# A hybrid layer stack on one core: GpSimd's clears and splits reordered, the rotation's sums moved to GpSimd

## The chip, the cores and the metric

The kernel runs on one core of one Trainium2 chip. The metric is the device time of one execution in microseconds. The engines are named as in the profile: PE is TensorE, PEld its weight load, DVE is VectorE, ACT is ScalarE, POOL is GpSimd and SP is SyncE, which issues all the transfers.

## The reference

The input x has 4 batches of 256 tokens with 256 channels. Four parts are added to it in turn, each computed from a layer norm of the current x:

```
x = x + attn_a(layernorm(x))     # 16 heads of 128, causal softmax attention with biases
x = x + ffn(layernorm(x))        # per-token int8 quantisation, product with an int8 256x256 weight
x = x + attn_b(layernorm(x))     # 16 heads of 128, 64 memory slots a head
x = x + ffn(layernorm(x))
```

attn_b works on rotated queries and keys. The rotation splits each head's 128 features in two halves:

```
rope(x) = concat(x1 * cos - x2 * sin, x2 * cos + x1 * sin)
s = clip(hs @ Ws1.T @ Ws2.T + bs2);  z = cumlogsumexp(s)
ok = exp(-z) * (tril(q k^T) @ exp(s));  qv = softmax(ok)
o = tril((qv * exp(-z)) @ exp(s)^T) @ v
out = (rmsnorm(o) * silu(g)) @ Wo.T
```

## The kernel before

Every engine has one instruction list written out by hand, and semaphores join the lists. So an instruction that waits holds up all that stand behind it on its engine. Heads are worked in 8 pairs. A loop over pairs (`Fori(0, PAIRS - 1)` with `a_body`, later with `b_body`) is followed by a last pair that is written out. Inside a body, b runs over the 4 batches, and while batch b's attention is computed, the projections for the other half of the tokens (512 tokens at a time) are put between its products as filler. Projections of q and k, and those of v and the gate in attn_b, are done in three products of split numbers: ACT writes the high part (`split_head`, line 530), POOL subtracts it from the raw weights for the low part (`split_tail`, line 380, and `split_out_tail`, line 385, for the output weights). For x the high part comes from ACT (`transposed`, line 537) and the low part from DVE (`tail`, line 820).

Four norms are numbered 0 to 3. DVE makes the statistics (`ln_stats`, 804 and 807), POOL the reciprocal root (`ln_rsqrt`, 372 and 374), DVE the scaled rows (`ln_scale`, 813). PE transposes them (`transpose_x`, 1199), and ACT copies the transposed rows out, first a plain copy (536), then the high part (537).

At the start POOL clears five buffers (`oT_hi`, `oT_lo`, `wo_hi`, `wo_lo`, `accT`, lines 401 to 407) just after the first low parts, while DVE scales batches 2 and 3 of norm 0. PE does the first of eight projection tasks, then transposes batches 2 and 3, then does the other seven. Between the two attentions POOL splits the weights of v and gate and clears `wo_hi`, `wo_lo` and `accT` again. Each ffn runs as `ffn_quant` (826 to 840), transposes (1212), a product (1221), `ffn_out` (849 and 855, which leaves float16 rows), and `ffn_add` on POOL (391).

The rotation in attn_b: ACT copies the projection with its two halves exchanged into `rot_s` (666, 667), POOL multiplies that by the sines in place (`rope_mul`, 439), DVE multiplies the projection in PSUM by the cosines into `rot` (`b_rope_cos`, 992), and DVE adds the two into qT or kT (`b_rope_add`, 999). `rot` and `rot_s` have one buffer for head 0 and one for head 1, shared by q and k. PE's next score products wait for all four sums of their phase (`b_rope`), and PE's reuse of a projection bank waits for the cosine product that reads it.

The gate's norm weight is folded into the output weights by ACT (`wos`, line 722). In the loop its low part is taken by POOL. In the last pair PE's `out_proj` (1371) multiplies by `wos` itself, after waiting for `b_wos`:

```
if last:
    pe.wait_ge(b_wos, PAIRS)
    out_proj(b_, b, wos)
```

Of the kernel before, what the change touches and what calls it, by code (L numbers as in the profile page):

```python
# [29 lines left out]
F32 = mybir.dt.float32  # L30
# [41 lines left out]
def layer_kernel(nc, x_in, a_wq, a_bq, a_wk, a_bk, a_wv, a_bv, a_wo, a_bo,  # L72
                 b_wq, b_wk, b_wv, b_wg, b_wo, b_ws1, b_ws2, b_bs2, b_gw,
                 f_w, f_ws, f_bias, consts, out):
    with ExitStack() as ctx:
# [111 lines left out]
        cast_done = sem("cast_done")  # L187
        gwh_done = sem("gwh_done")
# [173 lines left out]
        def _(pool):  # L362
# [3 lines left out]
            g.memset(ws2[:, :], 0.0).then_inc(init_done, 1)  # L366

# [31 lines left out]
            def zero_outputs():  # L399

                g.memset(wo_hi[:, :, :].bitcast(F32), 0.0)
                g.memset(wo_lo[:, :, :].bitcast(F32), 0.0)
                return g.memset(accT[:, :, :], 0.0)
# [24 lines left out]
            ln_rsqrt(2, 1)  # L428
            split_tail(b_, 0, 2)

            pool.wait_ge(a.y_acc, y_count(B - 1))
            zero_outputs().then_inc(b_.y_acc, 1)

            def rope_mul(n, m, k):
# [5 lines left out]
                                ).then_inc(b_rotmul, 1)  # L440

# [20 lines left out]
            def b_body(i, last):  # L462
                x = i * B
                for b in range(B):
# [4 lines left out]
                    if b % 2 == 0:  # L469
# [8 lines left out]
                        if rest:  # L478
                            rope_mul(n("q0"), 0, 0)
                            rope_mul(n("q1"), 0, 1)  # L480
                        if nxt:
                            slots(x + b + 1, (b + 1) % B)
                        if rest:
                            rope_mul(n("k0"), 1, 0)
                    else:
                        if last and b == 3:
                            ln_rsqrt(3, 2)
                        if rest:
                            rope_mul(n("k1"), 1, 1)
# [13 lines left out]
            for j, (m, k) in enumerate(((0, 0), (0, 1), (1, 0), (1, 1))):  # L503
                rope_mul(slot_done(0, 0, B_TASKS.index(ROPES[j])), m, k)
                if j == 0:
                    ffn_add(0, 2)
                if j == 1:
                    ffn_add(0, 3)
                    ln_rsqrt(2, 2)
                    ln_rsqrt(2, 3)  # L510
# [10 lines left out]
        def _(act):  # L521
# [10 lines left out]
            def transposed(m, b, bank):  # L532
# [3 lines left out]
                s.activation(xT[:, :, cols], src, ACT.Copy)  # L536
                s.activation(xT_hi[:, :, cols], src, ACT.Copy).then_inc(xts[m].hi, 1)

# [1140 lines left out]
```

## Time and profile before

| | us |
|---|---|
| median of 3 runs (lowest to highest) | 839.63 (838.05 to 842.48) |
| time of the profiled execution | 837.9 |
| its span | 836.1 |
| PE busy | 775.7 (93%) |
| DVE busy | 592.8 (71%) |
| ACT busy | 432.7 (52%) |
| POOL busy | 277.3 (33%) |

The span goes from the first instruction to the last one. Busy time is the share in which an engine executes; a busy PE is not necessarily at its highest clock. A line's time gives the start, then the duration.

### The profile page before, as it was taken

The page shows a single profiled execution, that of the slowest core. Times are in us where ns is not written, and L with a number is a line of the kernel's source. Part 1 is how long each engine was busy: PE and PEld are TensorE (multiplying, and loading weights), DVE is VectorE, ACT ScalarE, POOL GpSimd, SP SyncE. Part 2 cuts the span into 40 slices and gives each one's busy share as a digit, 9 for nine tenths or more (in the row PEclk, how much of TensorE's full clock was granted, in tenths as well). Part 3 has the DMA queues.
Part 4 walks back from the last instruction along what each step waited for, and adds up shares of the span by engine and source line. Part 5 has one row for each costly group of instructions (what it writes and reads, how often), then busy time and mean ns, then how long its engine had stood idle before and what let it go on. Part 6 is the DMA issues. An engine that isn't in the chain of part 4 may idle for free.

```text
span 836.1 us, 14186 instructions
## 1 busy us (share of the span) xinstructions
PE 775.7 (93%) x4428; PEld 655.5 (78%) x4428; DVE 592.8 (71%) x1500; ACT 432.7 (52%) x1184; POOL 277.3 (33%) x285
## 2 busy tenths in 40 slices
PE   3999999999999995689999999999999999999963
PEld 2788888888888884368888888888888888888752
DVE  6455554555555448888888878888888788887776
ACT  3555555555555543356656566565565665565320
POOL 6110010101001004535635446356354463553231
PEclk9999999999999999799999999999999999999996
DMA  7010101101010200100100101001001010000001
GB/s 246 1 51 0 50 12 38 50 0 50 0 50 12 63 1 13 51 2 13 51 1 13 50 1 63 0 13 50 0 13 50 12 50 0 13 0 0 1 1 51
DMA packets 23653, 23.74 MB, mean 28 GB/s; under 512 B 2369, under 2 KB 23361, under 8 KB 23506
## 3 DMA queue, kind: packets, MB, share of 16 engines
q1 hardware_dynamic: 23634, 23.51, 8.9%
q8 instruction: 10, 0.16, 0.1%
q14 instruction: 9, 0.07, 0.0%
HBM read 22.45 MB, written 1.05 MB: 28 GB/s over the span
## 4 chain that ended last, share of the span: by engine, by line
PE 87%; DVE 8%; ACT 1%; issue 1%; POOL 1%; DMA 1%; SPq 0%; ACTq 0%; DVEq 0%
PE ps L1247 21%; PE ps L1453 11%; PE ps L1354 6%; PE ps L1252 6%; PE ps L1275 5%; PE ps L1465 3%; PE ps L1318 3%; PE ps L1359 3%; DVE xn L813 3%; PE ps L1490 2%; PE ps L1294 2%; PE ps L1477 2%; PE ps L1507 2%; PE ps L1509 2%; PE ps L1508 2%; PE ps L1466 2%
## 5 line engine op out<-in xcount | busy, mean ns | idle before, releaser
L1247 PE MATMUL ps<-xT_hi,w_hi 128*128 128x512 f32 x256 | 110.2, 431 | 4.4 <-DVE rot L992 2.5
L380 POOL TENSOR_TENSOR w_lo<-w_raw,w_hi 128x512 fp32r<-128x512 f32 x32 | 40.7, 1282 | 217.3 <-ACT w_hi L530 217.3
L1247 PE MATMUL ps<-xT_hi,w_lo 128*128 128x512 f32 x256 | 101.6, 397 | 0.0
L1247 PE MATMUL ps<-xT_lo,w_hi 128*128 128x512 f32 x256 | 101.2, 395 | 0.0
L1022 DVE TENSOR_TENSOR wt<-ps,const 128x384 f32<-128x384 f32 x128 | 68.3, 555 | 41.8 <-PE ps L1466 21.9
L439 POOL TENSOR_TENSOR rot_s<-rot_s,const 128x512 f32<-128x512 f32 x64 | 81.9, 1291 | 16.1 <-ACT rot_s L667 16.1
L574 ACT ACTIVATE wt<-wt,negmax 128x128 f32<-128x128 f32 (+1 forms) x128 | 56.6, 443 | 36.1 <-DVE negmax L889 36.1
L877 DVE TENSOR_TENSOR v<-ps,bv_b 128x256 f32<-128x256 f32 x64 | 26.9, 422 | 59.5 <-PE ps L1252 59.4
L1252 PE MATMUL ps<-wv,xT 128*128 128x256 f32 x256 | 63.1, 380 | 1.0 <-DVE v L877 1.0
L686 ACT ACTIVATE v<-ps 128x256 f32<-128x256 f32 x64 | 24.4, 381 | 73.4 <-PE ps L1453 73.2
L1011 DVE RECIPROCAL enz<-zs 128x128 f32<-128x128 f32 x64 | 60.3, 942 | 0.0
L1247 PEld LDWEIGHTS ps<-xT_hi,w_hi 128*128 128x128 f32 x256 | 48.9, 191 | 13.9 <-issue 2.9
L1247 PEld LDWEIGHTS ps<-xT_hi,w_lo 128*128 128x128 f32 x256 | 48.7, 190 | 11.2
L459 POOL TENSOR_TENSOR qp<-oke,enz 128x256 f32<-128x256 f32 x32 | 23.6, 736 | 101.6 <-ACT oke L691 101.6
L1453 PE MATMUL ps<-wc_hi,xT_hi 128*128 128x512 f32 x128 | 56.5, 441 | 0.0
L884 DVE TENSOR_TENSOR wt<-ps,const 128x128 f32<-128x128 f32 x64 | 18.3, 286 | 53.1 <-PE ps L1275 53.1
L992 DVE TENSOR_TENSOR rot<-ps,const 128x512 f32<-128x512 f32 x64 | 43.6, 681 | 16.1 <-ACT rot_s L667 16.1
L1247 PEld LDWEIGHTS ps<-xT_lo,w_hi 128*128 128x128 f32 x256 | 49.1, 192 | 6.9
L666 ACT ACTIVATE rot_s<-ps 64x512 f32<-64x512 f32 x64 | 38.0, 594 | 30.1 <-PE ps L1247 27.6
L1453 PE MATMUL ps<-wc_hi,xT_lo 128*128 128x512 f32 x128 | 50.8, 397 | 0.0
L1453 PE MATMUL ps<-wc_lo,xT_hi 128*128 128x512 f32 x128 | 50.7, 396 | 0.0
L591 ACT ACTIVATE wt<-ps 128x384 f32<-128x384 f32 x64 | 30.1, 486 | 39.6 <-PE ps L1294 39.6
(160 smaller groups left out, 2140.8 us busy)
## 6 DMA issues: line engine op xcount, KB each, us to landing
w_raw<-a_w_q SPq DMA_DIRECT2D x8, 256.0 KB, 3.2
w_raw<-a_w_k SPq DMA_DIRECT2D x8, 256.0 KB, 3.8
wv<-a_w_v SPq DMA_DIRECT2D x8, 256.0 KB, 2.5
wo<-a_w_o SPq DMA_DIRECT2D x8, 256.0 KB, 3.3
w_raw<-b_Wq SPq DMA_DIRECT2D x8, 256.0 KB, 2.6
w_raw<-b_Wk SPq DMA_DIRECT2D x8, 256.0 KB, 3.3
wc<-b_Wv SPq DMA_DIRECT2D x8, 256.0 KB, 3.5
wc<-b_Wg SPq DMA_DIRECT2D x8, 256.0 KB, 4.0
```

Of the source, the lines that this page charges most:

```text
L380: g.tensor_tensor(lo[:, :, :], raw[:, :, :], hi[:, :, :].bitcast(F32), ALU.subtract).then_inc(ph.w_lo, 1)
L439: g.tensor_tensor(ap, ap, const[:, col:col + T].unsqueeze(1).to_broadcast([P, 2, T]), ALU.mult).then_inc(b_rotmul, 1)
L574: last = s.activation(wt[:, h, lo:hi], wt[:, h, lo:hi], ACT.Exp, bias=negmax[:, h, r:r + 1], scale=(1.0, -1.0)[r], accum_out=rowsum[:, h, ...
L666: s.activation(rot_s[0:M, k, :], PJ[bank][M:P, :], ACT.Copy)
L992: d.tensor_tensor(rot[:, k, :].rearrange("p (b t) -> p b t", b=2), PJ[n[0]].rearrange("p (b t) -> p b t", b=2), const[:, col:col + T].unsq ...
L1011: d.reciprocal(enz[:, HT * half + k, :], zs[:, k * P:(k + 1) * P]).then_inc(b_recip_done, 1)
L1022: d.tensor_tensor(dst, src[:, 0:384], tri3, ALU.mult).then_inc(done, 1)
L1247: ins = mm(PJ[n[0]], w[:, m, c, h * P:(h + 1) * P], x[:, c, cols], start=(t == 0), stop=(t == len(terms) - 1))
L1252: ins = mm(bank_ap, xT[:, c, tile * P:(tile + 1) * P], w[:, c, :], start=(c == 0), stop=(c == C - 1))
L1275: ins = mm(W_[h][:, lo:hi], qT[:, h, t0 + r * P:t0 + (r + 1) * P], kT[:, h, t0:t0 + hi - lo], start=True, stop=True)
L1354: mm(Y_, w[:, h, c * P:(c + 1) * P], oT_hi[:, half, h, :], start=(h == 0 and w is wo_hi), stop=False)
L1453: ins = mm(PJ[bank], x[:, c, tile], w[:, c, :], start=(c == 0 and t == 0), stop=(c == C - 1 and t == 2))
```

## The change

In words, by place:

- POOL at the start: `wo_hi`, `wo_lo` and `oT_hi` are cleared ahead of the first `ln_rsqrt`, `oT_lo` between the first two. `split_tail(a, 0, 0)` waits until DVE has scaled batches 0 and 1, `split_tail(a, 0, 1)` until all are scaled, and the clear of `accT` comes after it.
- The start on the other engines: ACT's plain copies of x leave `transposed` for norm 0 and come later (`x_copy`). DVE takes the low parts of batches 0 and 1 before the statistics of batch 3. PE does the four q and k projections without a break, then transposes batches 2 and 3. DVE takes their low parts between the evacuations of v.
- Between the attentions: POOL waits until six tiles of norm 1 are scaled before it clears `wo_hi` and `wo_lo`, and splits v's and gate's weights only after all of `ffn_quant(0, ...)`. `accT` is cleared after the first `slots`. Two `ffn_add` go from POOL to DVE (`add_ffn`), and DVE's list there is reordered.
- In attn_b's loop: the four sums of a phase go from DVE to POOL (`rope_add`), behind the sine products. DVE's and ACT's lists are reordered: `b_recip` of tile 0 moves to the odd steps, the exponential of `oke` goes ahead of k0 and et, the copy to `wos` goes behind k0, and the two weight splits of the odd step change places with squares and copies.
- At the end: `ffn_quant(1, 2)` is cut into `ffn_range` and `ffn_round` with the add of batch 3 and its statistics between, `ffn_out(1, 2)` goes behind `ffn_quant(1, 3)`, and POOL holds `ffn_add(1, 1)` until batch 2 is scaled.

The diff, cut to its core:

```diff
             g.memset(ws2[:, :], 0.0).then_inc(init_done, 1)
+            g.memset(wo_hi[:, :, :].bitcast(F32), 0.0)
+            g.memset(wo_lo[:, :, :].bitcast(F32), 0.0)
+            g.memset(oT_hi[:, 1, :, :].bitcast(F32), 0.0)
...
-            for b in range(B):
-                ln_rsqrt(0, b)
-                if b == 1:
-                    split_tail(a, 0, 0)
+            ln_rsqrt(0, 0)
+            g.memset(oT_lo[:, 1, :, :].bitcast(F32), 0.0)
+            ln_rsqrt(0, 1)
+            pool.wait_ge(norms[0].xn, 4)
+            split_tail(a, 0, 0)
+            ln_rsqrt(0, 2)
+            ln_rsqrt(0, 3)
+            pool.wait_ge(norms[0].xn, TILES)
             split_tail(a, 0, 1)
...
-            g.memset(oT_hi[:, 1, :, :].bitcast(F32), 0.0)
-            g.memset(oT_lo[:, 1, :, :].bitcast(F32), 0.0)
-            zero_outputs()
-            pool.wait_ge(norms[0].xn, TILES)
+            g.memset(accT[:, :, :], 0.0)
...
             ln_rsqrt(2, 1)
+            pool.wait_ge(norms[1].xn, 6)
+            pool.wait_ge(a.y_acc, y_count(B - 1))
+            g.memset(wo_hi[:, :, :].bitcast(F32), 0.0)
+            g.memset(wo_lo[:, :, :].bitcast(F32), 0.0)
+            pool.wait_ge(ffns[0].qb, B)
             split_tail(b_, 0, 2)
-            pool.wait_ge(a.y_acc, y_count(B - 1))
-            zero_outputs().then_inc(b_.y_acc, 1)
...
+            def rope_add(r1, k, m, half):
+                pool.wait_ge(b_rotcos, r1)
+                pool.wait_ge(b_rotmul, r1)
+                g.tensor_tensor((qT, kT)[m][:, k, half * HALF:(half + 1) * HALF], rot[:, k, :], rot_s[:, k, :],
+                                ALU.add).then_inc(b_rope, 1)
...
                             rope_mul(n("q0"), 0, 0)
                             rope_mul(n("q1"), 0, 1)
+                            rope_add(4 * phase + 1, 0, 0, 1 - b // 2)
+                            rope_add(4 * phase + 2, 1, 0, 1 - b // 2)
                         if nxt:
                             slots(x + b + 1, (b + 1) % B)
                         if rest:
                             rope_mul(n("k0"), 1, 0)
+                            rope_add(4 * phase + 3, 0, 1, 1 - b // 2)
+                            rope_mul(n("k1"), 1, 1)
+                            rope_add(4 * phase + 4, 1, 1, 1 - b // 2)
...
             slots(0, 0)
+            g.memset(accT[:, :, :], 0.0).then_inc(b_.y_acc, 1)
...
+            pool.wait_ge(norms[3].xn, 6)
             ffn_add(1, 1)
...
-                        if b == 0:
-                            act.wait_ge(b_.wo_ld, i * 16 + 16)
-                            s.activation(wos[:, :, :], wo[:, :, :], ACT.Copy, scale=gwh[:, 0:1]).then_inc(b_wos, 1)
...
-                        if rest:
-                            t("k0")
                         if nxt:
                             b_okexp_step(x + b + 1)
+                        if rest:
+                            t("k0")
+                        if b == 0:
+                            act.wait_ge(b_.wo_ld, i * 16 + 16)
+                            s.activation(wos[:, :, :], wo[:, :, :], ACT.Copy, scale=gwh[:, 0:1]).then_inc(b_wos, 1)
...
-            for b in range(2, B):
-                ln_stats(0, b, x_ld[b], 16)
-            for b in range(B):
-                tail(0, b, 2 + b)
-                if b == 1:
-                    ln_scale(0, 2)
-                    ln_scale(0, 3)
+            ln_stats(0, 2, x_ld[2], 16)
+            tail(0, 0, 2)
+            tail(0, 1, 3)
+            ln_stats(0, 3, x_ld[3], 16)
+            ln_scale(0, 2)
+            ln_scale(0, 3)
...
-                            b_recip(n(3), half, 0)
-                            b_rope_add(4 * phase + 1, 0, 0, half)
...
             b_clip_s(n0(0), 0)
             ffn_out(0, 2)
+            ffn_out(0, 3)
             b_rope_cos(n0(1), 0, 0)
-            ffn_out(0, 3)
+            b_recip(n0(3), 0, 0)
             b_rope_add(1, 0, 0, 0)
+            add_ffn(0, 2)
+            add_ffn(0, 3)
+            ln_stats(2, 2, ffns[0].acc, 3)
             b_rope_cos(n0(2), 1, 0)
...
-            ffn_out(1, 2)
+            ffn_round(1, 2)
             ln_scale(3, 3)
             ffn_quant(1, 3)
+            ffn_out(1, 2)
             ffn_out(1, 3)
...
             for j in range(NA):
-                if j == 1:
+                if j == 4:
+                    pe.wait_ge(x_plain, 2)
                     transpose_x(0, 2, 4)
                     transpose_x(0, 3, 5)
-                if j == 4:
-                    pe.wait_ge(xts[0].lo, 4)
                     a_scores(0, 0, [(0, 2), (1, 2)])
                 a_task((j % 2, j // 2, None), j, 0, 0)
+            pe.wait_ge(xts[0].lo, 4)
+            pe.wait_ge(x_plain, 4)
```

## Rows read from the trace of the kernel before

**Rows 1.** Busy time in one stretch: length, PE, PEld, DVE, ACT, POOL, then clock, DMA.
```profile
500.00:550.00 50.00, 49.92 (x315) 43.02 (x315) 40.78 (x85) 29.35 (x84) 24.45 (x24) 1.00 0.08 26
```

**Rows 2.** PE alone by stretch: length, busy time, granted clock, DMA share, GB/s.
```profile
21.00:22.00 1.00, 1.00 (x4) 0.50 0.00 0
...
336.00:338.00 2.00, 0.05 (x1) 0.50 0.00 0
...
358.00:360.00 2.00, 2.00 (x6) 0.50 0.01 4
```

**Rows 3.** Instructions in order of time at the start: start, duration, engine, line.
```profile
8.47 1.73 DVE L813 TENSOR_SCALAR xn<-acc,mv,rstd 128x256 f32<-128x256 f32 x2 [0.61 <-POOL rstd L374]
...
13.13 6.86 DVE L813 TENSOR_SCALAR xn<-acc,mv,rstd 128x256 f32<-128x256 f32 x4
...
17.08 1.81 POOL L403 MEMSET accT<- 128x2048 f32 x1
```

**Rows 4.** The chain that ended last, at the start and in the loop: start, duration, what.
```profile
19.41 1.76 PE ps L1199 x8
21.17 5.18 PE ps L1247 x18
...
27.20 0.91 PE ps L1275 x4
...
505.12 1.39 PE ps L1453 x6
...
532.65 1.39 PE ps L1453 x6
```

**Rows 5.** Instructions in order of time between the two attentions.
```profile
334.18 0.70 DVE L813 TENSOR_SCALAR xn<-acc,mv,rstd 128x256 f32<-128x256 f32 x2
335.49 6.06 DVE L813 TENSOR_SCALAR xn<-acc,mv,rstd 128x256 f32<-128x256 f32 x4 [0.60 <-POOL rstd L374]
...
347.67 0.69 DVE L1005 TENSOR_SCALAR clip_buf<-ps 128x512 f32<-128x512 f32 x1
...
353.02 1.50 DVE L855 TENSOR_TENSOR y<-y,fb_b 128x512 f16<-128x512 f32 x1
354.45 1.74 DVE L999 TENSOR_TENSOR qT<-rot,rot_s 128x512 f32<-128x512 f32 x1
...
338.64 1.80 POOL L403 MEMSET accT<- 128x2048 f32 x1
...
364.68 0.70 PE L1465 MATMUL ps<-qT,kT 128*128 128x256 f32 x2 [1.36 <-DVE kT L999]
```

**Rows 6.** Instructions in order of time in one half of a pair of the second loop.
```profile
502.56 0.69 DVE L999 TENSOR_TENSOR kT<-rot,rot_s 128x512 f32<-128x512 f32 x1
...
503.64 0.60 PE L1465 MATMUL ps<-qT,kT 128*128 128x256 f32 x2
...
518.89 2.52 POOL L439 TENSOR_TENSOR rot_s<-rot_s,const 128x512 f32<-128x512 f32 x2
524.93 0.74 POOL L459 TENSOR_TENSOR qp<-oke,enz 128x256 f32<-128x256 f32 x1 [3.53 <-ACT oke L691]
...
527.22 0.59 ACT L667 ACTIVATE rot_s<-ps 64x512 f32<-64x512 f32 x1
```

**Rows 7.** Instructions in order of time in the last pair's first step.
```profile
760.44 0.73 ACT L722 ACTIVATE wos<-wo,gwh 128x512 f32<-128x512 f32 x1
...
773.22 0.59 ACT L667 ACTIVATE rot_s<-ps 64x512 f32<-64x512 f32 x1
...
772.42 1.02 PE L1371 MATMUL ps<-wos,clip_buf 128*128 128x256 f32 x4
```

**Rows 8.** Instructions in order of time at the end.
```profile
817.58 1.57 DVE L813 TENSOR_SCALAR xn<-acc,mv,rstd 128x256 f32<-128x256 f32 x2
...
824.35 0.69 DVE L855 TENSOR_TENSOR y<-y,fb_b 128x512 f16<-128x512 f32 x1
...
831.20 0.88 DVE L849 SCALAR_TENSOR_TENSOR y<-ps,qsc,ws_b 128x256 f32<-128x256 f32 x2 [2.43 <-PE ps L1221]
```

More of the change, by code:

```diff
@@ L555, in _ @@
             transposed(0, 1, 3)
+            x_copy(0, 2)
+            x_copy(1, 3)
             act.wait_ge(bias_ld, 16 * 4)
@@ L625, in _ @@
                 a_qk((f % 2, f // 2, f + 1), A_TASKS[f], 0, 0)
-                if f == 0:
-                    transposed(0, 2, 4)
-                    transposed(0, 3, 5)
+            transposed(0, 2, 4)
+            transposed(0, 3, 5)
             a_exp_step(0)
+            x_copy(2, 4)
+            x_copy(3, 5)
             act.wait_ge(small_ld, 16 * 7)
@@ L746, in b_body @@
                             t("k1")
+                            t("c0")
+                        if last and b == 3:
+                            ffn_copy(1, 1)
                         if b == 1 and not last:
@@ L749, in b_body @@
                         if rest:
-                            t("c0")
                             t("c1")
-                        b_squares(x + b)
-                        if last and b == 3:
-                            ffn_copy(1, 1)
                         if b == 1 and not last:
@@ L757, in b_body @@
                             split_head(b_, i + 1, 0)
+                        b_squares(x + b)
                         if rest:
                             t("c2")
-                        if b == 1 and not last:
-                            split_head(b_, i + 1, 1)
                         act.wait_ge(b_ogt_ps, x + b + 1)
@@ L767, in b_body @@
                             s.activation(oT_hi[:, b // 2, :, (b % 2) * T:(b % 2 + 1) * T], src, ACT.Copy).then_inc(b_.o_hi, 1)
+                        if b == 1 and not last:
+                            split_head(b_, i + 1, 1)
+                        if nxt:
+                            b_okexp_step(x + b + 1)
                         if rest:
                             t("et")
-                        if nxt:
-                            b_okexp_step(x + b + 1)
             act.wait_ge(init_done, 3)
@@ L982, in _, with b_rope_cos @@
             tail(1, 0, ffns[0].banks[0])
+            tail(1, 1, ffns[0].banks[1])
             ffn_quant(0, 2)
-            tail(1, 1, ffns[0].banks[1])
             ln_scale(1, 3)
             ffn_quant(0, 3)
-            def b_rope_cos(n, k, m):
+            def b_rope_cos(n, k, m, phase=0):
                 dve.wait_ge(b_.proj_evac[n[0]], n[1] + 1)
+                if not (isinstance(phase, int) and phase == 0 and m == 0):
+                    dve.wait_ge(b_rope, 4 * phase + 2 * m + k - 1)
                 col = (K_QCOS, K_COS)[m]
@@ L1115, in b_body @@
                         if rest:
-                            b_rope_cos(n(5), 1, 1)
-                            b_rope_add(4 * phase + 4, 1, 1, half)
+                            b_gate(n(6), phase, 0, half)
+                            b_recip(n(3), half, 0)
                         if last and b == 3:
@@ L1120, in b_body @@
                         if rest:
-                            b_gate(n(6), phase, 0, half)
+                            b_gate(n(7), phase, 1, half)
                             b_recip(None, half, 1)
+                        if last and b == 3:
+                            ffn_out(1, 0)
                         if nxt:
                             b_scores(x + b + 1)
-                        if rest:
-                            b_gate(n(7), phase, 1, half)
-                        if last and b == 3:
-                            ffn_out(1, 0)
                         b_gated(x + b, b)
@@ L1135, in b_body @@
                             out_tail(b_, x + b, b, O_)
+                        if rest:
+                            b_recip(None, half, 2)
                         if last and b == 3:
@@ L1138, in b_body @@
                             ln_scale(3, 2)
-                            ffn_quant(1, 2)
-                        if rest:
-                            b_recip(None, half, 2)
+                            ffn_range(1, 2)
                         (add_y if last else add_group)(b_, x + b, b)
```

64 lines of the change are left out of this document (34 added, 30 removed).

## The prediction, made before the changed kernel ran

> **What bounds the kernel now.** I first read the busy time by stretch [rows 1]. In the second attention's loop PE is busy for 49.92 of 50 us while DVE has 40.78 and POOL 24.45. There PE's own work sets the time, and what is taken from DVE is worth nothing unless it closes a gap in PE. PE alone by stretch shows where it is otherwise [rows 2]: near 21 us it works at half the clock, near 336 us it stands, near 358 us it again works at 0.50, shortly after a stop of 2.5 us. So I read those places, the last pair and the end in order of time.
>
> At the start two scalings of the norm (line 813) take 1.73 us, and then four take 6.86 [rows 3]. Between the attentions two take 0.70 and four take 6.06 [rows 5]. The instruction is the same, so the long ones are not working but held. In both places POOL runs without a break beside them: at the start a weight split and then clears up to 17.08 + 1.81 = 18.89, in the middle a split and clears up to 338.64 + 1.80 = 340.44. The scalings end 1.1 us after POOL does, the time of the remaining ones. PE's transposes of batches 2 and 3 wait for them until 19.41 [rows 4]. So this wait is on the path twice. At the end two scalings take 1.57, with one POOL add beside them, and the two of batch 3 the same [rows 8].
>
> The Trainium skill ("SBUF — State Buffer", section "SBUF: two separate sides") has VectorE in a two-port mode and GpSimd share a port pair that is locked for a whole instruction. By that rule alone a scaling would wait for one POOL instruction at most. The trace agrees on the lock and not on the turn-taking: the scaling waited through six POOL instructions.
>
> **The start, -6.0 us.** POOL's clears go to where it idles, and the first split waits for the scalings.
> - The second pair of scalings takes 0.70 instead of 1.73: -1.0. One plain copy (0.60, as long as ACT's 0.59 in [rows 6]) leaves ACT's path to the second high part: together about -1.5, so PE starts its first projection at 11.75 instead of 13.27.
> - PE then does all 24 products of the four tasks without the stop up to 19.41. At the high clock six take 1.39 us (0.232 each); 18 took 5.18 [rows 4], partly at the low level. At the clock of 0.50 [rows 2] six would take 2.6 (0.43 each), not quite twice the 1.39. Before, about 12 of the 24 ran at the low level. I take 12 again: 12 x 0.43 + 12 x 0.232 = 7.9, so to 19.7, plus 0.9 for eight transposes: scores at 20.5 against 27.20, -6.7. With 9 low products it is -7.3, with all 24 low (10.3, and transposes of 1.76) -3.4.
> - The low parts of batches 2 and 3 now lie on DVE between the v evacuations (2 x 0.60), and the loop waits for ACT's last plain copy (0.60). That costs about 0.7 back: -6.0. POOL's second split ends near 15.7, before PE needs it near 17. The bias add on POOL (4.6 us) ends before the softmax's scalings.
>
> The bounds: -7, and -3.
>
> **Between the attentions, -3.0 us.** The four scalings shrink from 6.06 to 1.4, but the second batch still has to be transposed, copied twice and subtracted: the low part ends near 339.3, and two quantisations and a scaling (5.1 us) follow. The clip starts at 344.45 instead of 347.67: -3.2. Behind it both `ffn_out` now stand ahead of the first cosine, which then comes only 0.7 earlier (PE's k0 near 350.9 instead of 352.9). The reciprocal, the first sum, the two adds moved to DVE (0.6 each) and statistics put the q1 cosine near 354.8 to 355.4 instead of 356.11; PE's k1 waits for that, as before. But before, a `y` took 1.50 and the sum behind it 1.74 instead of 0.69 beside POOL's adds [rows 5]; without POOL's adds most of that goes. I arrive at the last sum near 361.5 and at scores at 361.7 instead of 364.68: -3.0. The bounds are -1 (PE's idle time before k1 grows to 3 us and the low clock holds longer) and -5 (the adds cost nothing). The clear of `accT` (1.8 us) after `slots` lies in POOL idle time: the first use is 10 us later.
>
> **The loop, -1.0 us.** DVE loses four sums of 0.69 a half, POOL gains four. The trace has no such sum on POOL; the nearest row is two sine products in 2.52, the same shape and two SBUF inputs, so 1.27 each, 5.1 a half [rows 6]. POOL's 24.45 of 50 [rows 1] becomes about 33.7. The dates in a half, which takes 532.65 - 505.12 = 27.53 [rows 4]:
> - Sine products end at 521.4, sums 1 and 2 at 524.0. The exponential now comes before k0 on ACT, near 523.0, so `qp` starts at 524.0 instead of 524.93. PE's transposes want it at 525.7, where before they lost about 0.1 us; over 15 halves that is up to -1.6.
> - k0's sine and sum end at 527.2. ACT's last exchange ends at 527.81, so k1's sine at 529.15, its sum at 530.4. On DVE it ended at 503.25 + 27.53 = 530.8. PE's scores come at 503.64 + 27.53 = 531.2. The slack is 0.8 us, against 0.4 before.
>
> DVE's other moves (recip 0, gates) fit in its idle time. What is queued behind the sums on POOL is `qp`, then `rms`, which waits for ACT's squares near 532.6. If the cover of 0.8 us were gone, each late 0.1 us would cost 1.5 over the loop. I take -1.0, between -2.5 and +3.
>
> By the Trainium skill ("GPSIMD Engine Reference", section "Engine selection") an elementwise operation with two inputs belongs on VectorE, being about 2x slower on GpSimd. The rows agree (1.27 against 0.69), yet by them POOL has the room.
>
> **The last pair, +2.1 us.** ACT's copy to `wos` (0.73) was done at 761.2, long before PE's output product at 772.42 [rows 7]. Now it stands behind k0's exchange, which ends at 773.22 + 0.59 = 773.8. The copy ends near 774.5, so that PE, which took no pause here, stands for 2.1 us. Behind it are k1 and c0 to c3, all dense PE work, so nothing absorbs it. In the loop the copy's readers come later, and it costs nothing. Bounds: +1.5 and, if the clock falls after this pause, +3.8.
>
> **The end, -3.0 us.** The scaling of batch 2 takes 0.72 instead of 1.57, as POOL's add waits: -0.85. That of batch 3 the same: -0.85. `ffn_out(1, 2)` took 0.88 + 0.69, less overlap 1.5, ahead of the last scaling [rows 8]; now it lies in the 2.43 us in which DVE waited for PE before 831.20. Against that, the add of batch 3 waits for PE's product, and the rounding goes behind the statistics: about +0.2. Sum -3.0, bounds -1.8 and -3.5.
>
> **The sum.** -6.0 - 3.0 - 1.0 + 2.1 - 3.0 = -10.9 us. The profiled execution took 837.9 (span 836.1, 1.8 around it), so 827.0. The median of the runs is 839.63, 1.7 above that execution: I predict 828.5.
>
> **Rivals.**
> 1. *The held scalings go, but little of it arrives* (chance 0.13). PE's clock stays low through all of the first 24 products, falls again in the pause before the first loop, and between the attentions the wait moves to k1. The low clock after such a stop is in the rows, at 358 us [rows 2]. Start -3, middle -1, loop 0, last pair +2.1, end -3: -4.9, so 834.7.
> 2. *POOL becomes late in the loop* (0.06), the case on the other side. It decides from the point where the last sum is more than 0.8 us late. The mechanism is the held port: DVE's `oke` subtraction has two SBUF inputs and falls at 522.1, between POOL's two sums. The rows show `y` stretched from 0.69 to 1.50 in such a meeting [rows 5]. If the subtraction waited for both sums, the exponential would come 1.8 us later, now ahead of k0, and k0, k1 and their sums as much: 1.0 us beyond the slack, 15 times, +15 us: 843.5. For it: the scaling at the start waited through six POOL instructions. Against it: `y`, the same kind as the subtraction, waited for one (0.8 longer, not more), and one sum leaves it within the slack.
> 3. *The change does nothing at its main places* (0.04): the long scalings have another cause, such as the transfers of the start, in flight until 19 us. Against it: from 336 to 338 us, inside the long scalings of the middle, no transfer runs [rows 2]. Only the last pair's cost and the end stay: 839.
> 4. *More than forecast* (0.07): 9 low products, the wait for k1 gone, all small gaps closed: -16: 823.5.
>
> The forecast has 0.70. The range of 823 to 834.5 holds it, rival 4 and half of rival 1. A difference of 0.5%, 4.2 us, is about what a measurement of this kernel can tell from none. Faster by more than that: the forecast, rival 4 and most of rival 1, 0.88. Within it 0.07, slower 0.05.
>
> **What would show it.** Start: four scalings of 0.35 to 0.4 near 12.5 to 14.3, scores near 20.5, PE dense before them. Middle: the four scalings in 1.4, the clip 3.2 earlier relative to the stage, the first scores 3.0. Loop: halves of 27.5; POOL sums of 1.27. Last pair: a PE wait of 2 us for ACT's `wos` at the output product. End: scalings of 0.7. The prediction is wrong if halves become longer than 27.7, if a scaling is still held by another POOL instruction, or if the clock is low when a loop begins.

## The result, and the profile after

| | before | after |
|---|---|---|
| median, us (lowest to highest) | 839.82 (838.05 to 842.48, 4 runs) | 829.92 (829.08 to 830.64, 4 runs) |
| span of the profiled execution | 836.1 | 827.0 |
| PE, DVE, ACT, POOL busy | 776, 593, 433, 277 | 776, 550, 436, 354 |

The ratio is 0.988, with a 95% interval of 0.985 to 0.991: faster by about 1.2%. PE is busy for the same 776 us, so in sum the 9.1 us of span are shorter pauses of PE.

The busy time of the stretch shown in [rows 1], now of the changed kernel: POOL has gone from 24.45 to 34.17 and DVE from 40.78 to 37.76, and PE is as full as before.

```profile
500.00:550.00 50.00, 49.93 (x305) 42.45 (x303) 37.76 (x78) 29.88 (x78) 34.17 (x31) 1.00 0.07 22
```

Instructions in order of time at the start, which answer to [rows 3]. The scalings of batches 1 and 3 take 0.74 and 0.73, as long as an undisturbed pair, and the split and the clear of `accT` begin behind them.

```profile
8.80 0.74 DVE L830 TENSOR_SCALAR xn<-acc,mv,rstd 128x256 f32<-128x256 f32 x2 [0.61 <-POOL rstd L378]
...
14.18 0.73 DVE L830 TENSOR_SCALAR xn<-acc,mv,rstd 128x256 f32<-128x256 f32 x2 [0.61 <-POOL rstd L378]
...
14.99 1.28 POOL L384 TENSOR_TENSOR w_lo<-w_raw,w_hi 128x512 fp32r<-128x512 f32 x1 [0.85 <-DVE xn L830]
16.21 1.81 POOL L407 MEMSET accT<- 128x2048 f32 x1
```

PE alone there. All 24 projection products run without a stop from 12.12 to 19.95, where before PE stood from about 16 to 19.41 [rows 4]. From 12.12 to 16.6 they follow each other every 0.43 us, the pace of the lower level (1.2 GHz), then every 0.23 (2.4 GHz). The last row shows what was given back: PE stands for 2.37 us before the loop, for ACT's last plain copy of x.

```profile
12.72 0.63 PE L1279 MATMUL ps<-xT_lo,w_hi 128*128 128x512 f32 x1
13.14 0.63 PE L1279 MATMUL ps<-xT_hi,w_lo 128*128 128x512 f32 x1
...
16.96 0.39 PE L1279 MATMUL ps<-xT_hi,w_lo 128*128 128x512 f32 x1
17.19 0.39 PE L1279 MATMUL ps<-xT_hi,w_hi 128*128 128x512 f32 x1
...
19.95 1.04 PE L1231 MATMUL ps<-const,xn 128*128 128x128 f32 x8
20.98 1.55 PE L1307 MATMUL ps<-kT,qT 128*128 128x128 f32 x8
22.36 3.62 PE L1284 MATMUL ps<-wv,xT 128*128 128x256 f32 x16
28.35 0.54 PE L1326 MATMUL ps<-const,wt 128*128 128x128 f32 x3 [2.37 <-ACT xT L551]
```

Between the attentions (to [rows 5]; the rows of one engine stand together). The four scalings take 1.38 instead of 6.06. But the first `y` is stretched, to 1.60: it now meets the split of `wc_lo`. The sum behind the second `y` is not held any more, 0.63 instead of 1.74. PE's wait before k1 has become 3.60, from 2.52.

```profile
331.59 1.38 DVE L830 TENSOR_SCALAR xn<-acc,mv,rstd 128x256 f32<-128x256 f32 x4 [0.61 <-POOL rstd L378]
...
340.24 0.68 DVE L1034 TENSOR_SCALAR clip_buf<-ps 128x512 f32<-128x512 f32 x1
...
341.74 1.60 DVE L879 TENSOR_TENSOR y<-y,fb_b 128x512 f16<-128x512 f32 x1
...
347.62 0.63 DVE L1028 TENSOR_TENSOR qT<-rot,rot_s 128x512 f32<-128x512 f32 x1
...
340.41 2.39 POOL L384 TENSOR_TENSOR wc_lo<-wc,wc_hi 128x1024 fp32r<-128x1024 f32 x1 [6.39 <-DVE qb L864]
342.75 1.74 POOL L451 TENSOR_TENSOR es_lo<-es,es_hi 128x512 fp32r<-128x512 f32 x1
...
351.05 0.47 PE L1279 MATMUL ps<-xT_hi,w_hi 128*128 128x512 f32 x1 [3.60 <-DVE rot L1021]
...
357.29 0.59 PE L1498 MATMUL ps<-qT,kT 128*128 128x256 f32 x2
```

In the second loop (to [rows 6]): two sums on POOL take 2.73, and the `oke` subtraction that meets them 0.73, where it takes 0.42 alone. Over the whole loop it takes 0.42 to 0.73, with a median of 0.57.

```profile
513.56 2.73 POOL L445 TENSOR_TENSOR qT<-rot,rot_s 128x512 f32<-128x512 f32 x2
514.40 0.73 DVE L1067 TENSOR_TENSOR oke<-ok,okmax 128x256 f32<-128x256 f32 x1
```

The last pair (to [rows 7]) and the end (to [rows 8]):

```profile
765.23 0.72 ACT L756 ACTIVATE wos<-wo,gwh 128x512 f32<-128x512 f32 x1
...
766.00 1.13 PE L1403 MATMUL ps<-wos,clip_buf 128*128 128x256 f32 x4 [2.30 <-ACT wos L756]
...
811.35 0.73 DVE L830 TENSOR_SCALAR xn<-acc,mv,rstd 128x256 f32<-128x256 f32 x2
...
822.07 0.88 DVE L873 SCALAR_TENSOR_TENSOR y<-ps,qsc,ws_b 128x256 f32<-128x256 f32 x2 [0.92 <-PE ps L1253]
```

**Where the 9.1 us of span came from.** I took the same instruction of both traces at each border, of PE where the table doesn't name DVE. "Gain" is how much shorter the piece is; each piece starts where the one above it ends.

| piece, up to | before, us | after, us | gain | forecast |
|---|---|---|---|---|
| first transposes (arrival of x) | 8.01 | 8.34 | -0.33 | 0 |
| first transposes of loop 1 | 33.32 | 28.35 | 5.30 | 6.0 |
| the last v products of attn_a | 307.29 | 302.39 | -0.07 | 0 |
| pair of scalings ahead of the four (DVE) | 334.18 | 330.28 | -1.00 | 0 |
| first q0 product of the loop of attn_b | 375.52 | 368.38 | 3.24 | 3.0 |
| last q0 product (14 halves) | 761.49 | 752.57 | 1.78 | 1.0 |
| first product with `wos` | 772.42 | 766.00 | -2.50 | -2.1 |
| last transposes of `og` | 814.57 | 808.28 | -0.13 | 0 |
| last addition (DVE) | 832.83 | 823.71 | 2.83 | 3.0 |

They sum to 9.12.

The 1.00 that was lost ahead of the scalings is PE's clock, and no edit of the change stands there. In both traces PE waits 2.4 us for DVE in attn_a's last pair. Behind this wait six transposes take 0.82 in the kernel before and 1.26 in the changed one:

```profile
321.97 0.82 PE L1294 MATMUL ps<-const,wt 128*128 128x128 f32 x6
```
```profile
317.06 1.26 PE L1326 MATMUL ps<-const,wt 128*128 128x128 f32 x6
```

The granted clock over the 4.2 us there (321.7 to 325.9, and 316.8 to 321.0) is 1.00 in the first and 0.59 in the second. In the thirteen other traces of this document, the changed kernel's among them, the piece from the last v products to this pair of scalings took 27.75 to 28.22 us. Only in the trace of the kernel before did it take 26.89, so that trace was lucky there.

### The profile page after: what moved, and what is told of

It is laid out like the page before. It is cut to its first block, busy times and chain, and to the rows that moved or that the text cites. A ratio compares the mean times of both kernels' runs of the same rounds, so it can differ in the third digit from the quotient of the medians.

```text
span 827.0 us, 14275 instructions
## 1 busy us (share of the span) xinstructions
PE 775.8 (94%) x4428; PEld 657.8 (80%) x4428; DVE 550.4 (67%) x1442; ACT 435.5 (53%) x1184; POOL 354.0 (43%) x343
## 4 chain that ended last, share of the span: by engine, by line
PE 90%; DVE 6%; ACT 1%; issue 1%; POOL 1%; DMA 1%; SPq 0%; DVEq 0%; ACTq 0%; POOLq 0%
PE ps L1279 22%; PE ps L1486 11%; PE ps L1284 6%; PE ps L1386 6%; PE ps L1307 5%; PE ps L1498 3%; PE ps L1350 3%; PE ps L1391 3%; PE ps L1326 3%; PE ps L1523 2%; PE ps L1510 2%; PE ps L1540 2%; PE ps L1542 2%; PE ps L1541 2%; PE ps L1499 2%; PE ps L1351 2%
## 5 line engine op out<-in xcount | busy, mean ns | idle before, releaser
L1284 PEld LDWEIGHTS ps<-wv,xT 128*128 128x128 f32 x256 | 45.1, 190 | 4.4
```

The lines of the kernel that those rows point to most:

```text
L1284: ins = mm(bank_ap, xT[:, c, tile * P:(tile + 1) * P], w[:, c, :], start=(c == 0), stop=(c == C - 1))
```

## The experiments

No kernel of this section leaves out any of the work. Medians are of each kernel's own runs, and ratios are against the kernel before on the same chip (its median was 840.18 beside the first four, 839.26 beside the next four, 838.36 beside the last four).

### The last pair: wos copied early (e1)

```
@@ ACT, b_body, even batches @@
                             split_head(b_, i + 1, 2)
+                        if b == 0:
+                            act.wait_ge(b_.wo_ld, i * 16 + 16)
+                            s.activation(wos[:, :, :], wo[:, :, :], ACT.Copy, scale=gwh[:, 0:1]).then_inc(b_wos, 1)
                         if rest:
                             t("s")
...
                             t("k0")
-                        if b == 0:
-                            act.wait_ge(b_.wo_ld, i * 16 + 16)
-                            s.activation(wos[:, :, :], wo[:, :, :], ACT.Copy, scale=gwh[:, 0:1]).then_inc(b_wos, 1)
```

> The changed kernel with one edit: the copy to wos stands where it did before the change, ahead of the s task. My theory: in the last pair PE's wait of 2.3 us for wos goes (its output product starts right behind k0), nothing else moves, so 829.9 - 2.4 = 827.5. Rival: the batch steps behind it are bound by other engines and absorb the wait, so the time stays at 829.9.

Measured: 827.36 us (826.54 to 828.37), ratio 0.985 (0.982 to 0.988). From the last q0 product to the first with `wos` it is 10.93 us, as in the kernel before, instead of 13.43. So the whole 2.5 us of that piece was this wait, and the median moved by as much (2.56). The theory holds, its rival fell.

### The sums back on DVE in the loop (e2)

```
@@ POOL @@
-                            rope_add(4 * phase + 1, 0, 0, 1 - b // 2)
-                            rope_add(4 * phase + 2, 1, 0, 1 - b // 2)
...
@@ DVE @@
                             b_rope_cos(n(2), 1, 0, phase)
+                            b_rope_add(4 * phase + 1, 0, 0, half)
...
+                            b_rope_add(4 * phase + 2, 1, 0, half)
```

The sums of k0 and k1 move in the same way.

> The changed kernel with the four rotation sums of the loop back on VectorE, at the places that they had; the rest of the new order stays. Theory: PE sets the loop and the 0.13 us that a half lost came from the earlier exponential and qp, so halves stay at 27.44 and the time at 829.9, within 1 us. Rival: the sums on GpSimd are what shortened the loop, so halves go back to 27.57 and the time to 831.7 or above.

Measured: 830.23 us (828.88 to 831.05). The 14 halves took 384.33 us, against 384.19 in the changed kernel and 385.97 before. The busy row of this kernel, in the columns of [rows 1], has DVE at 41.11 and POOL at 24.72, as before the change:

```profile
500.00:550.00 50.00, 49.93 (x306) 42.46 (x305) 41.11 (x86) 29.81 (x78) 24.72 (x24) 1.00 0.06 21
```

So sums on POOL give nothing and cost nothing. The loop's 1.8 us come from what else was reordered in it; in e3 below, where nothing in the loop is, it took 385.98. That this is the earlier exponential and `qp` is my reading of the traces and was not run alone.

### Only the clears and splits moved (e3), and only the new orders at the start (e4)

e3 is the kernel before with POOL's list changed outside the loops, at the start and in the middle:

```
             pool.wait_ge(init_done, 1)
-            for b in range(B):
-                ln_rsqrt(0, b)
-                if b == 1:
-                    split_tail(a, 0, 0)
-            split_tail(a, 0, 1)
...
+            pool.wait_ge(norms[0].xn, 4)
+            split_tail(a, 0, 0)
+            ln_rsqrt(0, 2)
+            ln_rsqrt(0, 3)
             pool.wait_ge(norms[0].xn, TILES)
+            split_tail(a, 0, 1)
+            g.memset(accT[:, :, :], 0.0)
...
-            split_tail(b_, 0, 2)
-
+            pool.wait_ge(norms[1].xn, 6)
             pool.wait_ge(a.y_acc, y_count(B - 1))
-            zero_outputs().then_inc(b_.y_acc, 1)
+            g.memset(wo_hi[:, :, :].bitcast(F32), 0.0)
+            g.memset(wo_lo[:, :, :].bitcast(F32), 0.0)
+            pool.wait_ge(ffns[0].qb, B)
+            split_tail(b_, 0, 2)
```

e4 is the changed kernel with POOL's list at the start as it was before.

> The kernel before with GpSimd's part alone, at the start and between the attentions: clears and splits moved, with their waits; no other engine's list changes. Theory of the prediction (the held scalings were on the path): start -4 (transposes of batches 2 and 3 behind the first projection at about 15.4 instead of 19.4), middle -2 to -3.5, in all 832 to 834. Rival (the orders of PE, ACT and DVE brought the gain): under 1.5 us faster than before, 838 or more.

> The changed kernel with GpSimd's list at the start as before the change: clears and splits again beside the scalings; the rest stays. Theory of the prediction: the held scalings are the price, start +4 to +5, so 834 to 835. Rival: PE now does its four q and k tasks first (until 20 us), so scalings held until 19 us are hidden behind them, and only the second pair of scalings (+1.0) is on the path: 831.

Measured: e3 831.86 us (830.08 to 832.51), ratio 0.991 (0.988 to 0.993); e4 831.3 us (830.12 to 832.4). The start of e3, in order of time, with nothing changed on PE, ACT and DVE:

```profile
11.76 1.37 DVE L812 TENSOR_SCALAR xn<-acc,mv,rstd 128x256 f32<-128x256 f32 x4
...
14.62 1.11 PE L1198 MATMUL ps<-const,xn 128*128 128x128 f32 x8
```

and that of e4, where the last two scalings are held as long as ever:

```profile
14.47 6.15 DVE L829 TENSOR_SCALAR xn<-acc,mv,rstd 128x256 f32<-128x256 f32 x2 [0.61 <-POOL rstd L375]
```

From the first transposes to the loop's first it took:

| POOL's list | old orders of PE, ACT, DVE | new orders |
|---|---|---|
| old | 25.31 (before) | 20.78 (e4) |
| new | 19.23 (e3) | 20.01 (after) |

My expectation of e4, 4 to 5 us lost, fell, and its rival's 831 came out: PE's new order does 24 products while the scaling is held, and so hides most of the 5.8 us of hold. Not all of e4's 1.4 us in the median need be the start's: in its trace PE's clock also fell in the last pair (see e5). In e3 the start gained 6.1 us, where I expected 4. Either remedy is enough, and the two don't add. The 0.8 between e3 and the changed kernel is no cost of the new orders that could be told from chance. With the new list of POOL, six traces with the new orders (the changed kernel, e1, e2, e5, e8 and e14) took 19.34 to 20.63 for this piece, and three with the old ones (e3, e10, e13) took 19.23 to 19.91.

In the middle most of the gain is the clears and splits too. From the pair of scalings ahead of the four to attn_b's first scores it took 30.50 us in the kernel before, 27.85 in e3 and 27.01 in the changed kernel. So POOL's list alone gains 2.65 there, and the other engines' new orders 0.84 more.

### What holds a scaling (e5, e6, e11, e12)

All four change POOL's list between the attentions. e5 is the changed kernel, e6, e11 and e12 the kernel before (in e5 the clear of `accT` behind `slots(0, 0)` goes, and e6 has a new semaphore `gap`; neither line is shown):

```
@@ e5: the clears beside the scalings, no split there @@
-            pool.wait_ge(norms[1].xn, 6)
             pool.wait_ge(a.y_acc, y_count(B - 1))
             g.memset(wo_hi[:, :, :].bitcast(F32), 0.0)
             g.memset(wo_lo[:, :, :].bitcast(F32), 0.0)
+            g.memset(accT[:, :, :], 0.0).then_inc(b_.y_acc, 1)
@@ e6: a gap behind each @@
             split_tail(b_, 0, 2)
+            pool.wait_ge(b_.w_lo, 3)
             pool.wait_ge(a.y_acc, y_count(B - 1))
-            zero_outputs().then_inc(b_.y_acc, 1)
+            g.memset(wo_hi[:, :, :].bitcast(F32), 0.0).then_inc(gap, 1)
+            pool.wait_ge(gap, 1)
+            g.memset(wo_lo[:, :, :].bitcast(F32), 0.0).then_inc(gap, 1)
+            pool.wait_ge(gap, 2)
+            g.memset(accT[:, :, :], 0.0).then_inc(b_.y_acc, 1)
@@ e11: a gap behind the split alone @@
             split_tail(b_, 0, 2)
+            pool.wait_ge(b_.w_lo, 3)
@@ e12: the clears first @@
-            split_tail(b_, 0, 2)
             pool.wait_ge(a.y_acc, y_count(B - 1))
             zero_outputs().then_inc(b_.y_acc, 1)
+            split_tail(b_, 0, 2)
```

> The changed kernel, with one thing put back between the attentions: GpSimd no longer waits for the norm's scalings, so three clears (two of about 0.52 us and accT's of 1.8 us) run back to back beside the four scalings of batches 2 and 3. Nothing is split beside them. Theory A (any GpSimd instruction holds a scaling, one that only writes too, and the scaling waits until the whole queue has run dry): the group of four scalings takes about 3.5 to 4.2 us instead of 1.38, and the time is 1.5 to 2.6 us above the changed kernel's. Rival B (a scaling is let in after the instruction that runs): the group takes 1.9 to 2.5, the time is about 0.5 us above. Rival C (only a weight split, which reads and writes SBUF, holds a scaling, and clears don't): the group stays at 1.38, no change.

> The kernel before, with the same work in the same order on GpSimd, but between the attentions each of its instructions (a weight split, then the three clears) begins only after the one ahead of it has signalled its end, so that there is a gap of some 0.1 us or less between them. Theory A (the scaling waits as long as GpSimd's instructions follow each other without a break, and gets in at the first gap): the group of four scalings takes about 3 to 4 us instead of 6.06, and the time is 1 to 2 us below the kernel before. Rival B (a gap of that size doesn't help, the scaling is held through the whole stretch): the group stays at about 6 us, and the time is the kernel before's within its error.

> The kernel before, with GpSimd waiting for its own split to end before the three clears between the attentions; the clears follow each other without a gap. In the kernel before the first of the four scalings took 5.10 us (until the last clear had ended) and the others 0.40 each. Theory A (what runs directly behind a split leaves no turn, but clears among themselves do, as in run e5, where four scalings took 0.69, 0.59, 1.97 and 0.40): the first scaling takes about 2.4 us, the next ones get in one behind each clear, the longest of them about 2 us, and the group ends near 5.5 us. Rival B (a queue without gaps leaves no turn, whatever is in it, and e5 was an accident of its timing): the first takes 2.4, the second about 2.9, the others 0.40, and the group about 6.1.

> The kernel before, with the three clears between the attentions ahead of the split instead of behind it, and no gap. Theory A (a scaling gets its turn between clears, and only the split with what follows it holds one for long): scalings of about 0.7, 0.6 and 2.0 us beside the clears, and the last held by the split for about 2.4, group about 5.7 us. Rival B (no turn in a queue without gaps): one scaling of about 5.1 us, three of 0.40, as in the kernel before. The whole time is that of the kernel before within 0.5 us in both.

The view of one tile gives the shortest, median and longest of the four scalings in ns, and when the first and the last started. In this order: before, e5, e6, e11, e12.

```profile
L813 DVE TENSOR_SCALAR xn<-acc,mv,rstd x4: 394/402/5097, 335.5 to 341.1; 128x256 f32<-128x256 f32 x4
```
```profile
L829 DVE TENSOR_SCALAR xn<-acc,mv,rstd x4: 395/637/1969, 331.0 to 334.0; 128x256 f32<-128x256 f32 x4
```
```profile
L819 DVE TENSOR_SCALAR xn<-acc,mv,rstd x4: 687/1330/2432, 337.1 to 340.7; 128x256 f32<-128x256 f32 x4
```
```profile
L814 DVE TENSOR_SCALAR xn<-acc,mv,rstd x4: 686/1326/2431, 336.6 to 340.1; 128x256 f32<-128x256 f32 x4
```
```profile
L812 DVE TENSOR_SCALAR xn<-acc,mv,rstd x4: 590/1327/2421, 336.0 to 339.0; 128x256 f32<-128x256 f32 x4
```

POOL beside them in e12. Two of the clears take 0.14 and 0.15 longer than the 0.52 and the 1.80 of the kernel before, where no scaling got in between; it looks as if they in turn waited a little for one:

```profile
335.95 0.52 POOL L401 MEMSET wo_hi<- 128x512 f32 x1
336.42 0.66 POOL L402 MEMSET wo_lo<- 128x512 f32 x1
337.02 1.95 POOL L403 MEMSET accT<- 128x2048 f32 x1
338.94 2.37 POOL L380 TENSOR_TENSOR wc_lo<-wc,wc_hi 128x1024 fp32r<-128x1024 f32 x1
```

One more place belongs here, in attn_a's last pair, and it is alike in every trace. Two scalings meet two splits that follow each other without a gap. This is the kernel before:

```profile
317.45 1.69 DVE L813 TENSOR_SCALAR xn<-acc,mv,rstd 128x256 f32<-128x256 f32 x2
...
317.67 2.59 POOL L380 TENSOR_TENSOR w_lo<-w_raw,w_hi 128x512 fp32r<-128x512 f32 x2
```

The second scaling was held for 1.37 in all, that is through the first split, and was done at 319.14, while the second split ran until 320.26.

Read together:
- A clear, which only writes, holds a scaling too. In e5 there is no split, and the scalings take 0.59, 0.69, 1.97 and 0.40.
- Between clears, between a clear and a split behind it (e5, e12), and between two splits, one scaling gets its turn, and is then held by the next instruction. There the rule of one instruction at most holds. In e12 the last scaling is held by the split alone (2.42).
- A scaling that is held by a split with a clear directly behind it gets no turn, not even between the clears that follow. In the kernel before one was held for 5.10, through the split and three clears, and then three passed at 0.40. At the start it was 5.90, through a split and five clears.
- A gap behind the split of 0.05 us (its signalled end) is enough to give the turn back. e11, with this gap alone, is like e6, with one behind each.

So theory A of e11 and e12 holds for the clears, though not in its general words: a second split directly behind a split did leave a turn. (There a scaling was already running when the first split began, so the two cases differ in that too.) In e6 a gap did let a scaling in, as theory A had it, but a gap is not needed between clears, and its numbers fell (a group of 3 to 4 us, and 1 to 2 us of time): the first gap lets one scaling in, not all, and the next clears hold the others. The group shrank only from 6.06 to 5.54, since each scaling still pays for the POOL instruction behind it. In e5 the scalings came in turns, as rival B had it, but with 3.40 neither its 1.9 to 2.5 nor the 3.5 to 4.2 of theory A came out. Only keeping POOL silent gives 1.38. Why a clear directly behind a split leaves no turn is open.

The Trainium skill ("SBUF — State Buffer", section "SBUF: two separate sides") has the shared pair held for the full instruction, with the other engine blocked. By that, the held scaling of 2.4 us in e6, e11 and e12 is one split of 2.35, and the runs agree; the 5.10 of the kernel before is more than it allows.

The times: e5 831.36 (830.92 to 833.36, 5 runs), e6 841.29 (835.05 to 843.08), ratio 1.001 (0.999 to 1.004), and e11 840.16 and e12 839.79 in a single run each, within the spread of the kernel before. In e6, e11 and e12 the group ended 0.5 to 0.6 us sooner, and yet attn_b's first scores came 31.4 to 31.6 us behind the pair of scalings ahead, against 30.50 in the kernel before. PE's second four products with `ws` ran at the low level there (1.89, against 1.04), so the clock took more than the group gave. In e5 the group is 2.0 us longer, but the loop of attn_b begins only 0.6 later, counted from the same pair: PE's wait before k1 shrank from 3.60 to 2.79. More of its 1.4 us in the median fits the last pair. There e5 has the same `wos` wait as the changed kernel, but the clock fell behind it. PE alone over the same 4 us, first in e5 (0.63), then in the changed kernel (1.00):

```profile
766.00:770.00 4.00, 3.81 (x14) 0.63 0.00 0
```
```profile
766.00:770.00 4.00, 4.00 (x22) 1.00 0.00 0
```

From the first product with `wos` to the next projection it took 4.30 us in e5 (766.19 to 770.49) and 2.64 in the changed kernel (766.00 to 768.64): 1.7 more. The second group of these products shows it alone, 1.91 in e5 and e4, 1.03 in e2, e8 and the changed kernel, all behind a pause of the same 2.3 to 2.6 us. What decides between them, these runs don't show.

### The split of wc_lo moved (e8), and all together (e10)

```
@@ e8, from the changed kernel @@
-            pool.wait_ge(ffns[0].qb, B)
-            split_tail(b_, 0, 2)
...
                 rope_mul(slot_done(0, 0, B_TASKS.index(ROPES[j])), m, k)
+                if j == 1:
+                    split_tail(b_, 0, 2)
```

e10 is e8 with the `wos` copy of e1 and, at the start, the old orders of PE, ACT and DVE.

> The changed kernel, with GpSimd's split of the second attention's third weight group (2.39 us, beside which VectorE's first y took 1.60 us and ScalarE's and GpSimd's next steps followed late) moved behind its first two sine products. Theory: y takes 0.69 again, the first sine products start about 0.9 us earlier, and the second attention's first scores come 0.5 to 1 us earlier: 829.2 to 829.4 where the changed kernel is at 829.9. Rival: the stretch only moves to another two-input VectorE instruction that now meets the split, or PE's wait for the rotation is set by something else: no change.

> All that the runs so far point to, in one kernel: the changed kernel's clears and splits, loop and end, with the wos copy ahead of the exchange of task s (run e1: -2.5 us), the split between the attentions behind the first two sine products, and at the start the orders of PE, ScalarE and VectorE as in the kernel before, with only the clears moved (run e3 reached the loop 0.8 us sooner after the first transposes than the changed kernel). If the three add up: 827.4 - 0.5 - 0.8, so 826.0 to 826.6. Rival: the clock takes the gains back (what PE does earlier at the start it does at the low level): 827.4, as run e1.

Measured: e8 831.43 us (830.27 to 833.0), e10 829.49 (828.22 to 829.88). Both expected times fell; what e8's rival named, that the stretch moves to another instruction, is what happened. The first `y` took 0.69, as I wanted. But the second, which now meets the first sine product, took 1.51, and the first sum of the rotation now meets the split and waits for all of it, 2.70 instead of 0.63, and PE's wait before k1 grows from 3.60 to 4.87. In e8:

```profile
346.68 2.70 DVE L1028 TENSOR_TENSOR qT<-rot,rot_s 128x512 f32<-128x512 f32 x1
...
346.46 2.37 POOL L384 TENSOR_TENSOR wc_lo<-wc,wc_hi 128x1024 fp32r<-128x1024 f32 x1
...
352.18 0.77 PE L1279 MATMUL ps<-xT_hi,w_hi 128*128 128x512 f32 x1 [4.87 <-DVE rot L1021]
```

From the pair of scalings ahead of the four to the first scores e8 took 29.71 against 27.01. The sum is on PE's path and `y` much less so. The stretch that I took for a loss in the changed kernel was the cheaper place.

### The old start orders with the early copy (e13), beside e1 again (e14)

e13 is e10 with the split of `wc_lo` where the change has it. e14 is e1's kernel unchanged.

> The changed kernel with the wos copy ahead of the exchange of task s (as run e1), and at the start the orders of PE, ScalarE and VectorE as in the kernel before, with only GpSimd's clears and split moved. The split between the attentions stays where the change has it, since moving it (runs e8 and e10) cost 1.5 to 2 us. The loop of the first attention should begin 0.4 to 0.8 us sooner after the first transposes than in e1 (19.5 or less instead of 19.95), and the middle should be as in e1: 0.4 to 0.8 us below e1, 826.6 to 827.0. Rival: it is lost again to the clock at one of the later pauses, as e1.

> The kernel of run e1 once more, unchanged, beside e13 on the same chip, since differences below 1 us are to be read: 827.4 if runs on different chips compare, and e13 0.4 to 0.8 below it.

Measured: e13 827.47 us (826.5 to 828.14), ratio 0.986 (0.984 to 0.988); e14 827.16 (826.08 to 828.9), ratio 0.987 (0.984 to 0.989). e14 repeats e1 within 0.2 us. From the first transposes to the loop e13 took 19.91 against 20.63, and up to attn_b's first scores it was 1.0 ahead (the 0.7 of the start lies within the spread of equal starts given at e4). But in the profiled executions it lost this at the end, where PE's clock was lower. PE alone over the last 42 us, e13 first (0.75), then e14 (0.85):

```profile
780.00:822.00 42.00, 26.12 (x138) 0.75 0.05 16
```
```profile
780.00:822.00 42.00, 23.66 (x144) 0.85 0.06 19
```

The expected 0.4 to 0.8 us did not come. The rival, lost to the clock, fits these two traces; that it explains the medians too isn't shown. The version to keep is e1: the changed kernel with the `wos` copy ahead of the exchange of `s`, 827.3 us. It is faster than the kernel before and the changed one, and e13 can't be told from it.

## Why the prediction was right, point by point

Forecast 828.5 in a range of 823 to 834.5, measured 829.92. The sign, the places and all five terms' signs were right. The sum was -10.9, the span moved by -9.1 and the median by -9.9. (By its own numbers, 827.0 and 1.7, the forecast should have read 828.7.) That the sum came so near is in part luck: the start and the last pair gave 1.1 less than forecast and the clock ahead of the scalings took 1.0, and the loop gave 0.8 more.

- **Start, -6.0 forecast, -5.3 measured** (and x came 0.33 later, which no term had). The price of the 24 products was right: 7.9 forecast, 7.83 measured, with about 11 at the lower pace where I took 12. Attn_a's first scores, forecast at 20.5, came at 20.98. What was too small is the part given back: I took 0.7 for ACT's last plain copy, and from the first scores to the loop it is 7.37 instead of 6.12, so 1.25. What e3 adds: the same gain comes with the clears alone, and the reordering of PE that I credited with the dense products is not needed for it.
- **Between the attentions, -3.0 forecast.** Counted from the pair of scalings ahead of the four, it was -3.5 up to the first scores and -3.2 up to the loop. Another 1.0 was lost just before, to the clock, which no term had; so the traces as a whole show -2.2. The scalings (1.4 against 1.38) were right. The clip came 3.5 earlier, against 3.2 in the forecast, and PE's k0 3.1 earlier, against 2.0. One step is half wrong, "without POOL's adds most of that goes": the sum's 1.74 became 0.63, but a `y` is stretched to 1.60 as before, by the split that the change moved there. And that sum had been held by a sine product of POOL (353.94 to 355.65), not by an add. PE's wait before k1, 3 us in my lower bound, became 3.60.
- **Loop, -1.0 forecast, -1.8 measured.** A sum takes 1.27 to 1.49 (1.27 forecast), and a half became 27.44 (27.57 before). No wait for a sum came about. The slack that I worked out was enough: e2 shows that the placing of the sums changes nothing. Rival 2 fell because the subtraction waited for part of one sum (0.73 at most, against 0.42), not for two.
- **Last pair, +2.1 forecast, +2.5 measured**, and e1 shows its cause. A clock that falls behind the pause, for which I gave an upper bound of 3.8, is in the traces of e4 and e5. In e5 it makes 4.2 of the term (2.5 and 1.7), so that bound was too low.
- **End, -3.0 forecast, -2.8 measured.** The scalings take 0.73 and 0.74 instead of 1.57 and 1.56. In e3, where the end is as before, this piece took 18.60 us (18.26 in the kernel before, 15.43 in the changed one), so the gain is the new orders'; no run takes its terms apart.
- **The hold.** That a scaling waits through a whole row of POOL instructions was right for both places, but not as a general rule, as e5, e12 and the two splits at 317.67 show.

The prediction named a clock that would be low when a loop begins as what could make it wrong. In this trace it was 1.00 in both loops.

## What to carry to other kernels

When a DVE instruction takes several times its usual duration, look at POOL in the same stretch before anything else. If POOL works, ask which DVE instructions will meet it after a move: moving the split off `y` put it on a sum that PE waits for, and cost 1.5 us (the medians of e8 against the changed kernel; 2.0 in e10 against e13). A copy that is made in every pass of a loop must be checked for the last pass by itself: 0.72 us of `wos` copy, harmless seven times, cost 2.5 us the eighth. And a hold can be removed (move the clears) or covered (give PE other work): here the first was worth 6.1 us and the second 4.5 at the start, both together no more.

## What the runs showed of the hardware

- A scaling on DVE (TENSOR_SCALAR, from SBUF to SBUF) was blocked by POOL's clears as well as by its splits. It got a turn after each clear, and between two splits that follow each other (1.37 us, one split of 1.32). With a clear directly behind the split it got none until POOL was done: 5.10 us through four instructions in the middle, 5.90 through six at the start. A gap of 0.05 us behind the split restored the turn.
- DVE's additions with two SBUF inputs waited for the end of the POOL instruction that ran (2.70 instead of 0.63 beside a split of 2.37), and one got in between two that follow each other: `y` ended at 343.34, and `es_lo`, started at 342.75, took 1.74 instead of 1.28.
- PE's clock after the same pause of 2.3 us was 1.00 in one kernel and 0.63 in another over the next 4 us. The 1.7 us that it cost are as much as the whole gain of the loop. After a wait of 2.4 us in attn_a's last pair it was 1.00 in the trace of the kernel before and 0.59 in that of the changed one, which cost 1.0. So a difference below 1 us between two single traces says nothing by itself, and a gain of that size at one place can't be counted on at the end.
- At the start the pace of the products and the granted clock's column disagree: they were 0.43 us apart from 12.12 to 16.6 while the column shows 1.00. In the kernel before they were as far apart from 21.4 to 22.7, where the column shows 0.50 up to 22. I went by the pace.
